# Half of the attention scores leaves PSUM through ACT and is masked on GpSimd, in a gated linear attention block with a mixture of experts

## What is computed

```python
def step(state, inp):
    qt, kt, vt, gt = inp
    gate = jnp.exp(gt)
    state = state * gate[..., None] + vt[..., None] * kt[..., None, :]
    out_t = jnp.einsum('bhvk,bhk->bhv', state, qt)
    return (state, out_t)
```

## Time and profile before

| | us |
|---|---|
| median of 3 runs | 1012.97 |
| lowest and highest run | 1010.79, 1014.01 |
| the profiled execution's own time | 1017.69 |
| span in its trace | 1015.8 |

### The profile page before, as it was taken

How to read it: one execution, slowest core, us unless ns; L and a number is a source line. 1 busy time by engine, 2 the same in 40 slices (tenths; PEclk the granted TensorE clock), 3 DMA queues, 4 the chain that set the end, 5 groups by cost and what they waited for, 6 DMA issues and landing times.

```text
span 1015.8 us, 23482 instructions
## 1 busy us (share of the span) xinstructions
PE 851.1 (84%) x7033; PEld 739.9 (73%) x7034; DVE 680.2 (67%) x1650; ACT 452.1 (45%) x1196; POOL 382.8 (38%) x401
## 2 busy tenths in 40 slices
PE   5888888878878788788732998999999998999992
PEld 4565666656656566566522998999999998999992
DVE  3377877877877877787662674767467476675851
ACT  1566566566556656656411433333333332333330
POOL 4124433433433433443320244343534434354433
PEclk9799999999999999999855998999999999999997
DMA  6311111111111111111113324242424224322222
GB/s 232 138 33 38 48 48 37 47 47 40 51 42 48 42 42 53 37 43 47 39 64 107 100 45 126 45 121 48 125 43 123 44 45 123 48 43 52 42 34 29
DMA packets 53188, 65.01 MB, mean 64 GB/s; under 512 B 5953, under 2 KB 48658, under 8 KB 53010
## 3 DMA queue, kind: packets, MB, share of 16 engines
q1 hardware_dynamic: 29906, 36.00, 10.9%
q0 software_dynamic: 13440, 18.36, 10.0%
q10 hardware_dynamic: 9792, 10.03, 3.5%
HBM read 39.47 MB, written 24.90 MB: 63 GB/s over the span
## 4 chain that ended last, share of the span: by engine, by line
PE 43%; DVE 20%; issue 15%; DMA 11%; ACT 6%; DVEq 2%; SPq 1%; ACTq 1%; POOL 1%; POOLq 0%
PE p_a L1093 22%; DMA out_dram<-host_n,tok 8%; PE p_cum L1093 6%; DVE w_hi L864 5%; PE p_qk L1093 4%; PE p_gz L1093 4%; PE p_v L1093 4%; DMA ln_host<-expert_rows 2%; PE p_qk L1112 2%; ACT acts L716 2%; DVE host_o L879 1%; DVE st_x L809 1%; DVE pick L962 1%; DVE o_tok L967 1%; PE p_a L1259 1%
## 5 line engine op out<-in xcount | busy, mean ns | idle before, releaser
L634 POOL DMA_INDIRECT out_dram<-host_n,tok x72 | 148.0, 2055 | 265.6 <-DMA out_dram<-host_n,tok 184.6
L1093 PE MATMUL p_a<-w_hi_r,acts_r 128*128 x1152 | 209.6, 281 | 2.8 <-POOL w_lo_r L646 2.6
L1093 PEld LDWEIGHTS p_a<-w_hi_r,acts_r 128*128 128x128 f32 x1152 | 179.5, 189 | 3.4 <-issue 3.4
L1093 PE MATMUL p_a<-w_lo_r,acts_r 128*128 x576 | 161.6, 281 | 0.0
L771 ACT ACTIVATE x_host<-p_a,mods 128x256 f32<-128x256 f32 x72 | 36.8, 562 | 195.8 <-PE p_a L1259 194.5
L1093 PEld LDWEIGHTS p_a<-w_lo_r,acts_r 128*128 128x128 f32 x576 | 109.0, 189 | 0.0
L586 POOL TENSOR_TENSOR ln_host<-w_parts,gam 128x256 f32<-128x256 f32 x32 | 23.1, 722 | 208.8 <-DVE w_parts L910 208.8
L1055 DVE CAST acts_r<-acts 128x2048 fp32r<-128x2048 f32 x36 | 45.2, 1254 | 75.7 <-ACT acts L762 75.4
L611 POOL DMA_INDIRECT expert_rows<-rows,pos x64 | 64.7, 1010 | 54.2 <-DVE pos L978 31.9
L1057 DVE TENSOR_TENSOR acts_r<-acts,acts_r 128x2048 fp32r<-128x2048 f32 x36 | 82.5, 2292 | 1.2
L864 DVE TENSOR_TENSOR w_hi<-p_a,upto 128x1024 f32<-128x1024 f32 x64 | 75.2, 1216 | 0.3 <-PE p_a L1093 0.3
(11 more groups left out here) (204 smaller groups left out, 1913.2 us busy)
## 6 DMA issues: line engine op xcount, KB each, us to landing
w<-in_L_ffn_W_dram SPq DMA_DIRECT2D x16, 1024.0 KB, 7.7
ln_host<-expert_rows ACTq DMA_DIRECT2D x36, 272.0 KB, 3.0
host_x<-in_L_attn_x_dram SPq DMA_DIRECT2D x64, 128.0 KB, 2.1
out_dram<-x SPq DMA_DIRECT2D x32, 128.0 KB, 1.7
expert_rows<-pad_rows SPq DMA_DIRECT2D x16, 136.0 KB, 1.7
acts<-in_L_wmod_dram SPq DMA_DIRECT2D x1, 1536.0 KB, 6.5
out_dram<-host_n,tok POOLq DMA_INDIRECT x72, 4.4
b_all<-in_L_ffn_b_dram SPq DMA_DIRECT2D x1, 1024.0 KB, 7.6
```

Source lines behind the costliest of these rows:

```text
L634: nc.gpsimd.indirect_dma_start(out=out, out_offset=bass.IndirectOffsetOnAxis(ap=tok[u][:, h:h + 1], axis=0), in_=y_out[u][:, h, :], in_off ...
L1093: return nc.tensor.matmul(dst, lhsT, rhs, start=start, stop=stop, skip_group_check=True)
```

## The change

The second half of the scores no longer goes through DVE's mask. ACT copies it raw from PSUM into `am[:, 1]` after DVE has done mask 0, and GpSimd then applies the causal mask in place in SBUF by `affine_select`, which keeps an element where query minus key is not negative and writes zero elsewhere. Two semaphores are new: `raw_taken` (the copy is done; GpSimd waits for it, and TensorE before it writes p_w) and `am1_ready` (the select is done; TensorE waits for it ahead of output block 1).

```diff
@@ GpSimd, first in step
+                if back:
+                    wait_apart(pool, (raw_taken, s + 1))
+                    nc.gpsimd.affine_select(out=am[:, 1], in_=am[:, 1], compare_op=ALU.is_ge, fill=0.0,
+                                            base=0, pattern=[[0, HB], [1, P]], channel_multiplier=-1).then_inc(am1_ready, 1)
@@ ACT, between h2T and Abs
+                if back:
+
+                    act_e.wait_ge(a_ready, s + 1)
+                    after(act_e, o_ready, s)
+                    act_e.wait_ge(am_ready, s + 1)
+                    A.copy(am[:, 1].rearrange("p (b h) t -> p b h t", h=2),
+                           p_a[:, :, D:2 * D].rearrange("p b (h t) -> p b h t", t=P)).then_inc(raw_taken, 1)
@@ DVE
                 if back:
                     mask(0)
-                    mask(1)
@@ PE, ahead of the transposes into p_w
-                        pe.wait_ge(am_ready, KD * (s + 1))
+                        pe.wait_ge(am_ready, s + 1)
+                        pe.wait_ge(raw_taken, s + 1)
                     transposes(p_w, o_ln, KD, owT_ready)
@@ PE, the output blocks
-                    pe.wait_ge(am_ready, KD * (s + 1))
+                    pe.wait_ge(am_ready, s + 1)
                     output_of_block(0)
+                    pe.wait_ge(am1_ready, s + 1)
                     output_of_block(1).then_inc(o_ready, 1)
```

More of the change, by code:

```diff
@@ L325, in build @@
         am_ready = sem("am_ready")
+        raw_taken = sem("raw_taken")
+        am1_ready = sem("am1_ready")
         o_ready = sem("o_ready")
```

## The result

| | before | after |
|---|---|---|
| median, lowest and highest of 20 runs each, us | 1013.25 (1007.9 to 1023.59) | 1020.05 (1012.32 to 1026.43) |
| time of the profiled execution, us | 1017.69 | 1024.88 |
| span in its trace, us | 1015.8 | 1023.2 |

The ratio is 1.0068, 95% interval 1.0041 to 1.0095: the change costs 6.8 us. The forecast was no change (+1.3 us, 1014.3), and the time lies 1 us above the stated range.

The account below looks back on a forecast made before the run. The loop was taken as bound by hand-overs: DVE's masks, o_ln and statistics, then ACT's mv_x. +1.3 (ACT queue) + 0.9 (TensorE wait) + 0.1 (step 30) - 1.05 (step 31) = +1.3, so 1014.3 us, range 1009.5 to 1019.0.

Parts of the forecast that it names:

- The loop's mechanism: Attention loop, ahead of mv_x: DVE wait gone, an equally long ACT queue in its place; +0.08 us odd, 0 even steps.
- all that follows keeps its distance to mv_x: Attention loop, behind mv_x: a later or earlier mv_x moves the rest of the step by the same amount.
- The copy: ACT, ahead of Abs: one copy of 128x1024 from PSUM, taken as 1.015 us, from 1.25 to 2.27 after mask start.
- The overlap of Abs with its tail: ACT's queue: Abs starts 0.10 us before the copy ends, at 2.17 instead of 1.52 after mask start.
- rival A: Loop, slower: ACT queue longer than the DVE queue it replaces; +0.22 odd, +0.14 even, sum +5.3, 1018.3 us; chance 0.25.
- The hand-over from DVE to ACT: Between mask 0's end on DVE and ACT's copy: about 0.04 us, taken from DVE's and ACT's mv_x.
- TensorE's additional wait: TensorE, between the output blocks: one more passed wait, 0.03 us a step, 0.9 us over 29 steps.
- The select: GpSimd, 128x1024 in SBUF: 1.05 us, from 2.7 to about 3.8, hidden before its reader at 7.95.
- Rival C: Loop, slower: select takes the two-input price and blocks DVE's standardising, 0.5 us in 16 odd steps, 1022 us; chance 0.04.
- Step 31: Last loop step, no front part: o_ln ends 1.14 us earlier, TensorE's transposes start at about 501.6, gain 1.05 us.
- rival D: Step 31, a little faster: TensorE's clock doesn't fall there, some 3 us, 1011 us; chance 0.05.
- the change touches only the first: Of the two stages, only the attention loop of 32 steps, ending near 500 us, is touched by the change.

Follow-up runs that it names:

- e12: Changed kernel with the w2_lo subtraction on DVE, ACT copying two of the four banks in all steps but step 0; one run, 985.56 us.
- e17: Changed kernel, w2_lo subtraction on DVE, DVE also masking banks 0 and 1 of the second half, ACT and GpSimd taking the other two; 988.47 us.
- e11: Kernel before with the w2_lo subtraction on DVE and the second mask left out in all steps but step 0; one run, 980.35 us.
- e6: Changed kernel with the w2_lo subtraction moved from GpSimd to DVE; 997.07 us, ratio 0.9811 to the kernel before.
- e5: Kernel before with the w2_lo subtraction moved from GpSimd to DVE; 995.3 us, ratio 0.9793 to the kernel before.
- e16: Changed kernel with one more wait, so GpSimd's w2_lo subtraction starts only after DVE's host_n pair; 1011.98 us, ratio 0.9956.
- e15: Kernel before with one more wait, so GpSimd's w2_lo subtraction starts only after DVE's host_n pair; 1012.14 us, ratio 0.9963.
- e3: Kernel before with one small GpSimd memset more at the head of each step with a back part; 1014.46 us, ratio 0.9962.
- e9: Kernel before with one short DVE instruction more (some 0.33 us) between the loop and the expert stage; 1011.61 us, ratio 0.9977.
- e10: Changed kernel with nine short DVE instructions more (some 3 us) between the loop and the expert stage; 1023.86 us, ratio 1.0071.
- e13: Kernel before with the change made in step 31 alone; 1017.94 us, ratio 1.0041.
- e14: Kernel before with the change made in every step but step 31; 1023.14 us, ratio 1.008.
- e1: Kernel before with GpSimd's w2_lo subtraction cut into four instructions of 128x512; 1018.85 us, ratio 1.0026.
- e7: Kernel before with the w2_lo subtraction on DVE and the qk copy put ahead of mv_x on ACT; 1006.0 us.
- e18: As e17, but with mask 0 cut in two so that ACT's copy need not wait for all of it; 990.05 us.

## Why the prediction was wrong, and where it was right

- **The loop's mechanism: right.** A full copy on ACT takes the place of DVE's second mask, and mv_x is no earlier. e12 and e17 confirm that the lengths of the two queues decide, down to mv_x at 3.65; e11 shows that below it an odd step gains nothing more. The forecast that all that follows keeps its distance to mv_x holds nearly: mv_x is 0.15 later in odd and 0.07 in even steps, the steps 0.10 and 0.03.
- **The copy**: 1.015 predicted, 1.015 measured. The overlap of Abs with its tail: 0.10 predicted, 0.11 measured. The worst end of rival A did not come.
- **The hand-over from DVE to ACT**: mis-sized. I took 0.04 from DVE's mv_x; behind the mask it is 0.11 (mask ends at 1.22, copy starts at 1.33). Every later ACT time is 0.07 later than forecast: mv_x 4.08, not 4.01.
- **TensorE's additional wait**: 0.03 a step predicted, nothing measured (blocks and sums 0.98 and 0.99 apart, together 1.97 as before). That was 0.9 us too much, and the ACT queue's part, by the longer hand-over, some 0.6 too little: the loop from mask 0 to mask 31 takes 2.0 us more, where my terms up to there gave 2.3. The agreement is partly luck.
- **The select**: 1.05 predicted, 1.10 measured, from 2.69 to 3.79 after the mask; nobody waits. Rival C is out.
- **Step 31**: the transposes come 0.93 us earlier after the mask (at 2.49 instead of 3.42), predicted 1.05. What they waited for last was the copy and not o_ln:

```profile
503.99 0.41 PE L1124 MATMUL p_a<-ident,host_o 128*128 128x128 f32 x2 [3.04 <-ACT w_hi L711]
```

The clock also fell later, as in rival D, but only delayed. Counted from the mask, it fell after 1.9 us before (0.55 in the stretch 501 to 502, so at 501.1) and after 2.9 us in the changed kernel (0.71 in 504 to 505, so at 504.4):

```profile
504.00:505.00 1.00, 0.54 (x3) 0.30 (x3) 0.00 (x0) 0.37 (x1) 0.98 (x2) 0.71 0.11 39
```

Together step 31 and what follows it gave back 1.85 us in the profiles, where the sum had 1.05.
- **The step that failed: "the change touches only the first" stage.** The sum took the expert stage's difference as nothing, without a reason from a row. The sum for the loop was +1.3, and in the traces the loop's last scatter comes 0.4 us later; where the meetings are gone, the change costs +1.8 (e6 against e5) and -0.2 (e16 against e15). The other 5 to 7 us arise in a stage whose instructions are the same, where w2_lo stops a host_n pair oftener, TensorE is idle longer for it (+3.9 us in the profiles), and is busy longer with the same matmuls (+2.4), its clock falling oftener. The pair's rows, the load of rows that ACT issues only after the pair (3 late ones before, 5 after), and the two removals agree on it; the count of stopped pairs goes with the stage's length but doesn't give it by itself. Each count is from one trace of a kernel; that the runs of the group are those with more stopped pairs is argued from the removals, not seen run by run. I had read the port rule for one new instruction (the select), not for the long GpSimd instruction that was there already.
- **The scatter**: the forecast's own range rested on three runs, 1010.79 to 1014.01. The kernel before really spreads from 1003 to 1024; three runs couldn't show that.

**What stays open**: why the change moves the order at w2_lo so often to the bad side. The traces show a difference of tenths of a us between two engines at tile 7. It is not GpSimd's code length (e3), not the start time alone (e9; e10 leaves it a part), and not one part of the change alone (e13, e14). The traces show falls of TensorE's clock in the stage, but not whether they come before the bad order or after it. Where the code of DVE, ACT and TensorE lies was not tried.

## What to carry to other kernels

In this loop offloading paid only up to the point where the receiving queue, in order, reaches the next shared hand-over as late as the giving one: compute both queues to that point, and size the piece so that they meet there. A long GpSimd instruction beside short DVE ones is a lottery in any stage; look for it before trusting a prediction of a few us, since a change elsewhere can turn the draw, and remove it first. What a stopped instruction costs is decided in the queues that wait for it: here a load that goes out 3 us later goes out behind larger ones and lands 5 us later than that. If the runs of the kernel spread over 1% on one core, ask what race makes them spread before pricing the change.

## What was not expected of the hardware

- One GpSimd subtraction of 128x2048 (4.6 to 5.1 us) stops DVE's host_n pair or cast for nearly its whole length. Moved to DVE, the eight instructions take 2.29 us each, TensorE is never idle in the stage, the program is 20 us shorter, and nearly all of the scatter is gone (e5).
- Cut into four, back to back, it stopped a pair for 5.13 us at one place and for 2.97 at another (e1).
- A stopped host_n pair moves a 272 KB load of rows behind two weight loads of 1 MB each: it then lands after 7.2 to 8.7 us instead of some 3, and TensorE waits for it. In each of the six traces with seven stopped pairs there are five such loads, in before three, in e9 two, in e5, e6, e15 and e16 none.
- A shorter step can be slower: in e7 a 1.29 us pause of TensorE, 0.60 before, went ahead of a fall of the clock to half, and scores that take 1.15 us took 2.09.
- A copy of 128x1024 over four PSUM banks costs ACT 1.015 us, one of 128x512 over two banks 0.59; a select costs GpSimd 1.10 us for 128x1024, and for 128x512 0.65 (e17) and 0.76 (e18), medians.
